# First dense half in loops of four groups: x loaded twice into four buffers each, g copied in the step of its product, gathered rows stored first

## What is computed

```
h = jnp.maximum(_layernorm(x, axis=-1), 0.0)
x = x + _L0_gnn_ref(h, ...)      # three times: h = h @ W_self.T + b_self + h_neigh @ W_neigh.T
                                 # (relu after the first two)
h = jnp.maximum(_layernorm(x, axis=-1), 0.0)
x = x + _L1_gnn_ref(h, edge_attr_128, ...)
# in L1:  h = (ho @ W_O.T + b_O + hi @ W_I.T + b_I + node_embs @ W_S.T + b_S) / 3.0
```

## Time and profile before

| | us |
|---|---|
| median of 3 runs | 7257.24 (7256.88 to 7260.77) |
| profiled execution | 7259.3 |
| its span | 7257.6 (granted TensorE clock 0.801) |
| first half, beside `positions` | 201 to 557 |
| second half, beside `lookup` | 557 to 932 |
| third half, `take` 1 | 1810 to 2213 |
| fourth half, `take` 2 | 2424 to 2827 |

### The profile page before, as it was taken

The page is one execution under the profiler, slowest core; times in us unless marked ns, Lnnn a source line. Parts: engine busy times, 40 slices in busy tenths (PEclk is TensorE's granted clock), DMA queues, the critical chain, the costliest instruction groups (busy, mean ns, idle before and its releaser), DMA issues. The chain is left out here.

```text
span 7257.6 us, 107414 instructions
## 1 busy us (share of the span) xinstructions
PE 4886.5 (67%) x23937; PEld 3569.4 (49%) x23937; DVE 3986.4 (55%) x14866; ACT 2906.5 (40%) x6394; POOL 4063.4 (56%) x4659
## 2 busy tenths in 40 slices
PE   4776735558687687733655636699999978844553
PEld 2454524335565466633553324476666644434553
DVE  5665646654564455743323205566999989843210
ACT  0565634433463364323101100246888855533000
POOL 0655556630550353666565660475888877655556
PEclk9998867779899898865788877557999989955766
DMA  2233346659458655954546537443444444434443
GB/s 84 95 109 101 108 148 192 193 170 326 142 179 273 199 175 186 293 161 135 157 145 140 103 43 227 139 129 133 172 170 171 170 138 146 122 105 123 79 70 47
DMA packets 1124775, 1088.58 MB, mean 150 GB/s; under 512 B 106450, under 2 KB 986241, under 8 KB 1124197
## 3 DMA queue, kind: packets, MB, share of 16 engines
q1 hardware_dynamic: 983746, 911.02, 39.7%
q0 software_dynamic: 140800, 175.08, 11.3%
HBM read 651.65 MB, written 456.06 MB: 153 GB/s over the span
## 5 line engine op out<-in xcount | busy, mean ns | idle before, releaser
L1058 POOL DMA_INDIRECT G_x<-node_table,G_idx x400 | 398.5, 996 | 165.6 <-issue 130.0
L1058 POOL DMA_INDIRECT G_V<-layer_rows,G_idx x400 | 380.6, 952 | 149.0 <-issue 107.3
L1911 PE MATMUL bank<-O_r,O_eq 125*125 125x128 f32 x1600 | 289.6, 365 | 242.2 <-ACT O_out L1937 209.5
L1088 PE MATMUL bank<-first_last_indicators,G_V 125*128 (+1 forms) x1600 | 282.0, 298 | 239.6 <-DVE G_V L1737 151.0
L1070 POOL DMA_INDIRECT out<-O_out,O_idx x200 | 315.8, 1579 | 215.5 <-DMA out<-O_out,O_idx 154.5
L1417 PE MATMUL bank<-B_S,B_V 127*128 127x125 f32 x2000 | 317.8, 302 | 156.8 <-DVE B_S L1405 107.4
L1070 POOL DMA_INDIRECT node_table<-H_out,H_idx x200 | 319.8, 1599 | 169.4 <-DMA node_table<-H_out,H_idx 114.0
L1911 PEld LDWEIGHTS bank<-O_r,O_eq 125*125 125x125 f32 x1600 | 282.2, 278 | 249.6 <-issue 168.8
L1055 POOL COPY G_idx<-i_tb 128x4 int32<-128x4 int32 (+1 forms) x100 | 18.7, 187 | 687.1 <-POOLq L255 523.7
L1088 PEld LDWEIGHTS bank<-first_last_indicators,G_V 125*128 125x128 f32 x1600 | 276.3, 260 | 249.9 <-issue 169.5
L1417 PEld LDWEIGHTS bank<-B_S,B_V 127*128 127x128 f32 x2000 | 276.8, 210 | 192.4 <-issue 122.5
(11 more groups left out here) (472 smaller groups left out, 15868.5 us busy)
## 6 DMA issues: line engine op xcount, KB each, us to landing
P_x<-node_table SPq DMA_DIRECT2D x196, 512.0 KB
B_V<-values SPq DMA_DIRECT2D x250, 256.0 KB
B_krow<-keys_dst SPq DMA_DIRECT2D x250, 250.0 KB
values<-G_V SPq DMA_DIRECT2D x200, 256.0 KB
BN_g<-node_table SPq DMA_DIRECT2D x195, 256.0 KB
out<-P_out SPq DMA_DIRECT2D x195, 256.0 KB
node_table<-G_xg SPq DMA_DIRECT2D x97, 512.0 KB
layer_rows<-A_a SPq DMA_DIRECT2D x100, 256.0 KB
```

The lines of the kernel that those rows point to most:

```text
L1058: pool.indirect_dma_start(out=rows[u % len(rows)][:, c, :], out_offset=None, in_=table, in_offset=bass.IndirectOffsetOnAxis(ap=idx[u % len ...
L1088: last = nc.tensor.matmul(m.bank[7][:, bass.ds((i * TILE + c) * 2, 2)], V[0:EP, c, :], m.ind[0:EP, bass.ds(i * TILE + c, 1), :].rearrange( ...
L1911: last = nc.tensor.matmul(m.bank[2 + u % 2][0:EP, d * D:(d + 1) * D], eq[u][:, c, d * EP:(d + 1) * EP], r[u][:, c, :], start=(c == 0), sto ...
```

## The change

- The loops of the four halves have bodies of 4 steps (unroll 4, back 7, ahead 4): the loop has steps 8 to 43 (nine passes), and some 17 steps are written out.
- x has 4 slots for statistics and n1, loaded four steps ahead as soon as n1(i) is done. The residual add reads a second copy `xr`, with 4 slots, which SP loads one step ahead when x1(i-3) is done. That is one more load of 256 KB a group, 196 loads or 50 MB in all.
- `xg` has 4 slots: x1(i-2) waits for the store of group i-6.
- Product g, its copy and the store come one step earlier (i-4 for i-5), so the last step is n+3 for n+4, and ACT's wait for product g before `hT` is gone.
- In both takes `idx`, `V` and their semaphores have 4 slots: POOL waits for store and product of group i-4.
- On SP the edge part (in the takes the store of V) stands ahead of the dense part in each step.

```diff
-        x = [sb(f"x{k}", [128, TILE, D]) for k in range(8)]
+        x = [sb(f"x{k}", [128, TILE, D]) for k in range(4)]
+        xr = [sb(f"xr{k}", [128, TILE, D]) for k in range(4)]
...
-        xg = [sb(f"xg{k}", [128, TILE, 2 * D]) for k in range(8)]
+        xg = [sb(f"xg{k}", [128, TILE, 2 * D]) for k in range(4)]
...
-        FIRST, START, LAST = -5, -2, n + 4
+        FIRST, START, LAST = -4, -2, n + 3
...
-                if has(i + 5):
+                if has(i + 4):
+                    if has(i):
+                        sp.wait_ge(s_n1, i + 1)
+                    sp.dma_start(x[u][:], x_dram[bass.ds(base_of(i + 4), ROWS), :].rearrange("(p j) f -> p j f", j=TILE)).then_inc(s_x[u], 16)
+                if has(i + 1):
+                    v = (u + 1) % 4
                     if has(i - 3):
-                        sp.wait_ge(s_n1, i - 2)
                         sp.wait_ge(s_x1, i - 2)
...
+                    sp.dma_start(xr[v][:], x_dram[bass.ds(base_of(i + 1), ROWS), :].rearrange("(p j) f -> p j f", j=TILE)).then_inc(s_xr[v], 16)
...
                 if has(i - 2):
-                    v = (u - 2) % 8
+                    v = (u - 2) % 4
                     dve.wait_ge(s_C, i - 1)
-                    if has(i - 10):
-                        dve.wait_ge(s_st[v], slot_value(i - 10, v, 8))
-                    nc.vector.tensor_tensor(xg[v][:, :, 0:D], pC[:].rearrange("p (j f) -> p j f", j=TILE), x[v][:], ALU.add)\
+                    dve.wait_ge(s_xr[v], slot_value(i - 2, v))
+                    if has(i - 6):
+                        dve.wait_ge(s_st[v], slot_value(i - 6, v))
+                    nc.vector.tensor_tensor(xg[v][:, :, 0:D], pC[:].rearrange("p (j f) -> p j f", j=TILE), xr[v][:], ALU.add)\
...
-                    if has(i - 6):
-                        act.wait_ge(s_G, i - 5)
                     evac(hT[p][:], pT2[:], ACT.Copy, s_T2, i - 4, s_h)
...
-                if has(i - 5):
-                    evac(xg[(u - 5) % 8][:, :, D:2 * D], pG[:].rearrange("p (j f) -> p j f", j=TILE), ACT.Copy,
-                         s_G, i - 5, s_g, scale=1.0 / 3.0)
+                if has(i - 4):
+                    evac(xg[u][:, :, D:2 * D], pG[:].rearrange("p (j f) -> p j f", j=TILE), ACT.Copy,
+                         s_G, i - 4, s_g, scale=1.0 / 3.0)
...
-    def sweeps(eng, own, other):
-        together(eng, ([own(eng)] if own else []) + ([other(eng)] if other else []), unroll=8, back=10, ahead=5)
+    def sweeps(eng, own, other, first_other=False):
+        together(eng, ([other(eng)] if other and first_other else []) + ([own(eng)] if own else []) + ([other(eng)] if other and not first_other else []),
+                 back=7, ahead=4)
...
-            sweeps(sp, dense.sync, sync)
+            sweeps(sp, dense.sync, sync, first_other=True)
...
-        idx = P.slots("idx", [128, TILE], I32, count=8)
-        V_whole, V = gathered(P, "V", count=8)
+        idx = P.slots("idx", [128, TILE], I32)
+        V_whole, V = gathered(P, "V")
...
-                f.landed(s_vo, i - 8, u)
-                f.after(s_hl, i - 8)
+                f.landed(s_vo, i - 4, u)
+                f.after(s_hl, i - 4)
```

More of the change, by code:

```diff
@@ L347, in __init__ @@
         pT1, pA, pB, pC, pG, pT2 = m.bank[0:6]
-        s_x = P.sems("d1_x_in", 8)
-        s_st = P.sems("d1_xg_out", 8)
+        s_x, s_xr = P.sems("d1_x_in"), P.sems("d1_x_again")
+        s_st = P.sems("d1_xg_out")
         s_n1, s_n2 = P.sem("d1_n1"), P.sem("d1_n2")
@@ L387, in body @@
                 if has(i + 2):
-                    w = (u + 2) % 8
-                    dve.wait_ge(s_x[w], slot_value(i + 2, w, 8))
+                    w = (u + 2) % 4
+                    dve.wait_ge(s_x[w], slot_value(i + 2, w))
                     for j in range(TILE):
@@ L415, in body @@
                     for j in range(TILE):
-                        last = nc.vector.tensor_scalar(n1[q][:, j, :], x[(u + 1) % 8][:, j, :], rs[q][:, 4 + j:5 + j],
+                        last = nc.vector.tensor_scalar(n1[q][:, j, :], x[(u + 1) % 4][:, j, :], rs[q][:, 4 + j:5 + j],
                                                        nb[q][:, 4 + j:5 + j], ALU.mult, ALU.add)
@@ L421, in body @@
                     for j in range(TILE):
-                        last = nc.vector.bn_stats(st[p][:, j, :], xg[(u - 2) % 8][:, j, 0:D])
+                        last = nc.vector.bn_stats(st[p][:, j, :], xg[(u - 2) % 4][:, j, 0:D])
                     last.then_inc(s_st1, 1)
@@ L460, in body @@
                     for j in range(TILE):
-                        last = nc.scalar.activation(n2[q][:, j, :], xg[(u - 3) % 8][:, j, 0:D], ACT.Relu, scale=rs[q][:, j:j + 1],
+                        last = nc.scalar.activation(n2[q][:, j, :], xg[(u - 3) % 4][:, j, 0:D], ACT.Relu, scale=rs[q][:, j:j + 1],
                                                     bias=nb[q][:, j:j + 1])
@@ L506, in body @@
                     nc.tensor.matmul(pA[:], m.w["self1"], h0T[p][:], start=True, stop=True).then_inc(s_A, 1)
[L507 to L510, removed]
+                if has(i - 4):
+                    pe.wait_ge(s_h, i - 3)
+                    if has(i - 5):
+                        pe.wait_ge(s_g, i - 4)
                     for j in range(TILE):
-                        last = nc.tensor.matmul(pG[:, j * D:(j + 1) * D], hT[q][:, j * 128:(j + 1) * 128], m.w["S"],
+                        last = nc.tensor.matmul(pG[:, j * D:(j + 1) * D], hT[p][:, j * 128:(j + 1) * 128], m.w["S"],
                                                 start=True, stop=True)
@@ L1531, in body @@
                     f = Flow(sp, has)
-                    v = (u - 1) % 8
+                    v = (u - 1) % 4
                     f.landed(s_g, i - 1, v, 64)
@@ L1542, in body @@
                     f.landed(s_g, i - 1, u - 1, 64)
[L1543 removed]
+                    first_last_sums(nc, m, V[(u - 1) % 4], i - 1).then_inc(s_hl, 1)
             return 1, n, n, 0, body
```

16 lines of the change are left out of this document (6 added, 10 removed).

## The result

The kernel after takes 7169.0 us (median of 4 runs, 7161.8 to 7176.7) against 7257.1 us (7256.1 to 7260.8): a ratio of 0.9878, 95% interval 0.9861 to 0.9895, or 88 us less. The profiled execution took 7174.6 us, its span is 7172.9 us at a granted clock of 0.806. I had forecast 7232 in a range of 7195 to 7310: the direction was right, and the gain three times what I had worked out.

A forecast was written before the change was run, and what follows sets the result against it. It took the halves to be bound by PE, ACT and DVE hand-overs, slowed while POOL issues indirect DMAs. Takes -22, product g -4, loops -3 and back-edges +2 gave -27 us from 7259.3, so 7232 us, range 7195 to 7310.

The forecast's parts named there:

- What bounds the halves: In the four halves, a chain of PE, ACT and DVE hand-overs, each step 1.7 to 2.8 us slower while POOL issues.
- The start of the takes: First two residual adds of each take: 11.6 us apart for 33.0, as in the lookup, so -21.4 us a take.
- r, the steps after it: Time per step between residual adds later in each take: 7.4 us for 43 steps, +10.5 us a take.
- Rival D: Takes' steps at 7.1 us with a pausing POOL: 7206 us, or 7190 with the start at 5.45; chance 0.12.
- The store of V first: On SP in the takes: zero, since the gather has mostly landed and the loads behind the wait have time.
- Rival B: Gathers cost the same wherever they lie, so the middle gives back the start's gain: 7248 to 7266 us; chance 0.25.
- Rival C: Slower: four slots of `xg` and twice the loads, with stores landing late beside POOL: 7296 or 7360 us; chance 0.23.
- `xg` slots: Four slots, x1(i-2) waiting for the store of group i-6: zero, upper bound 0.4 us on 160 steps.
- First half: Should change by 1 us only; more than 5 us would mean a part set to zero has a price.
- loops of four: Shorter loop bodies: -3 us in the second half alone, and +2 us for 24 more back-edges in all.
- The step less at the end of a half: Product g a step earlier saves one step of copy and store: -1.0 us a half, -4 us (0 to -8).

## Why the prediction was wrong, and where right

- **What bounds the halves: right, but half read.** I had the 33 us at the start, the slow steps beside POOL's issue and "remote". What I took for a price per step (1.7 to 2.8 us) comes from hand-overs that wait for the end of a burst. I had the rows of both places and did not put PE's ends beside POOL's.
- **The start of the takes: mechanism right, size off.** Term: -21.4 us in each take, from the lookup's 11.6 us. Measured: 5.1 and 5.5 us for 33.0, so -27.9 and -27.5, at my own lower bound of -27.5. The lookup was the wrong neighbour, which is 13 us of the miss.
- **r, the steps after it: wrong sign.** Term: 43 steps at 7.4, +10.5 us a take. Measured from the second add to the last: 322.8 us (1840.4 to 2163.2) for the 329.5 of before, -6.7. Take 2 gives 322.1 for 329.3, -7.2. Rival D had r = 7.1 and came closest, in part by luck: its reason, a POOL that pauses, is the part of the lead, and with the lead alone r stays at 7.6 (chip 6). Its lower end is misadded (7206 less 2 x 6 us is 7194, not 7190), and either lies above the 7169. The term is out by 17 us in each take, 34 in all.
- **The store of V first: the step that failed.** Term: zero. I asked only if something behind SP's wait would come late. I didn't ask who waits for the store itself: POOL, by the earlier trace rows, 62.2 us in 23 waits. I had even used that row as an argument that nothing would change. Alone it is 0.9922 on chip 5, with even steps of 7.05 us. On the first chip the order was never run alone; there the even steps, the same wait of POOL (48.3 us in 37 waits, none for a store of V) and the -7 us from the second add on in place of +10.5 are seen in the kernel after only.
- **Rival B: wrong.** The gathers don't cost the same wherever they lie. Over a free step of 5.45 us, a burst costs 1.6 us where one falls in each step (7.09 us), and 3.1 us where nine followed each other at the start (33.0 us).
- **Rival C and `xg` slots: no cost to be seen in the takes.** In the kernel after the DMA share in the middle of take 1 is 0.70 for 0.53 and the steps are shorter. The Trainium skill's rule that transfers of all issuers interleave on the same engines ("DMA: Bandwidth & Descriptors", section "Issuing engines are not separate DMA queues") isn't contradicted, but 0.70 leaves room. The second load alone is 0.9998 and 1.0002.
- **First half and loops of four: sign wrong.** I had said that more than 5 us in the first half would mean a price on a part set to zero. The phase is 3.1 us longer, and its last residual add comes 5.1 us later (548.1 for 543.0). I had -3 for the loops in the second half, which is 7.6 us longer. On chip 6 two runs with the same code in that half differ by 20 us (390.4 and 410.6), so the first result alone couldn't show it; but chip 14, where nothing is held up, has the same +5 and +7 us in these halves, and in the first of them looped steps that are slower than written-out ones. The 6.88 against 7.34 us of the earlier trace rows, from which I took the -3, came from places that differ in POOL's work.
- **The step less at the end of a half: -4 us, not contradicted** (-3 and -7 us for g a step early alone, at the edge of noise). The last two copies of the first half are 2.7 us apart in the kernel after:

```profile
553.79 0.58 ACT L444 ACTIVATE positions_xg<-bank 128x512 f32<-128x512 f32 x1
...
556.48 0.60 ACT L444 ACTIVATE positions_xg<-bank 128x512 f32<-128x512 f32 x1 [1.25 <-PE bank L514]
...
560.81 0.19 POOL L1058 COPY es_i_pos<-es_i_row 128x4 int32<-128x4 int32 x1 [53.22 <-POOLq L255]
```

- **Where the miss lies.** Of the 58 us between the forecast of -27 and the profile's -85, 34 are r, 13 the start of the takes and 29 the phases whose code is the same; the first two halves, longer and not shorter, go the other way. Without those 29 us the time would have lain just inside the range (7198 for 7195), so leaving it took both the wrong term and something that the terms don't speak of.
- **Not explained.** 29 us of the 85 between the two spans lie in phases whose code is the same. On chips 5 and 6 the piece after the takes varies between 4406 and 4429 us over six kernels that don't touch it, so a difference of 19 may well be that; it was not tested. Nor was it run what makes the kernel after 0.19% slower on chip 14: it isn't the second load alone, the lead, the order or g; the loops of four account for the first half by the traces, and for the rest they and the four slots of x and `xg` are left.

## What to carry to other kernels

When an engine is released by a transfer, ask where in its queue that transfer is issued, not only what stands behind its wait: moving one transfer on SP took POOL's release from a place that drifted to one that is fixed in the step, and on chip 5 that was worth at least as much as the shorter lead on chip 6. Give the issuer of gathers only the lead it needs, released by the engine it disturbs, so that it pauses once in each step. And compare on more than one chip where such an effect is the whole of a gain: this one is a gain of 1.2% on some and a loss of 0.2% on another.

## What the runs showed of the hardware

- **Held-up hand-overs.** On the chip of the first result and on chips 5 and 6, many of PE's hand-overs to ACT, DVE and POOL that fall into a burst of four indirect DMAs take effect about 0.9 to 1.3 us after the burst's last issue ended, 2 us and more after PE's work (1972.48 to 1974.49): 68 of 69 in the even steps of the kernel after, 16 of 52 in the uneven ones before, where 30 were taken within 0.9 us. With nine bursts in a row the dense chain stood for 33 us. Neither what holds them up nor what lets the others through is shown.
- **It isn't so on every chip.** On chips 14 and 15 the same instructions (a mean of 951 to 956 ns for one issue on all of them) hold up nothing (0 of 51 such hand-overs between 1690 and 1850 us in the run with lead and V first on chip 15), the steps of the takes are 5.4 us and the kernel before takes 6841 to 6846 us: 411 to 416 us less than on the first chip. What in the chips differs, no run here shows.
- **The clock beside it.** In the takes the granted clock was 0.94 with uneven steps and 1.00 with even ones, at the same work. Of its two levels, 1.2 and 2.4 GHz, the lower one no longer occurs in the middle of take 1; which idle time of PE had brought it on was not tested, and what part of the step's 7.33 to 7.09 us is the clock's own isn't separated from that of the rhythm.
- 50 MB more of loads beside 0.5 of DMA share cost nothing that 10 runs could see (0.9998 and 1.0002).
